# A GNN stack on one core: SpMM units cut into quarters between build batches, and zero fills issued by GpSimd

## The reference

```python
h = features * norm_out[:, None]
h = h @ W
agg = jax.ops.segment_sum(h[edge_src], edge_dst, num_segments=N)
gcn_out = agg * norm_in[:, None] + b
```

## Time and profile before

| | us |
|---|---|
| runs (3) | 2879.76, 2882.3, 2882.7; median 2882.3 |
| profiled execution, its span | 3131.6 |
| first build matmul to last SpMM matmul, in the profile | 88 to 503 |
| mean granted TensorE clock over the span | 0.771 |
| TensorE busy, share of the span | 69% |

### The profile page before, as it was taken

The page is one execution under the profiler, slowest core; times in us unless marked ns, Lnnn a source line. Parts: engine busy times, 40 slices in busy tenths (PEclk is TensorE's granted clock), DMA queues, the critical chain, the costliest instruction groups (busy, mean ns, idle before and its releaser), DMA issues.

```text
span 3131.6 us, 33483 instructions
## 1 busy us (share of the span) xinstructions
PE 2171.3 (69%) x10859; PEld 1508.0 (48%) x10859; DVE 1424.4 (45%) x3094; ACT 961.2 (31%) x2148; POOL 1362.2 (43%) x1417
## 2 busy tenths in 40 slices
PE   4899999468777777545666676682443443489998
PEld 3566667257666666332333333352333332356666
DVE  6766663646665655633444444332222222431414
ACT  3523321422233332553433443241222222220302
POOL 3000000666666663466666665257666666300000
PEclk9777778767888887768888888695555555599999
DMA  9479862277777885125666676314444554456361
GB/s 217 126 268 317 280 210 73 85 198 227 223 226 224 231 226 146 26 62 168 215 210 218 196 216 202 115 44 100 117 116 110 120 125 105 142 168 197 116 202 48
DMA packets 518583, 517.97 MB, mean 165 GB/s; under 512 B 153344, under 2 KB 463763, under 8 KB 517227
## 3 DMA queue, kind: packets, MB, share of 16 engines
q1 hardware_dynamic: 310349, 267.63, 28.1%
q0 software_dynamic: 50528, 115.22, 14.6%
q10 hardware_dynamic: 157534, 132.98, 13.7%
HBM read 301.53 MB, written 227.32 MB: 169 GB/s over the span
## 4 chain that ended last, share of the span: by engine, by line
PE 38%; another core or an unknown queue 15%; issue 14%; POOL 11%; DVE 9%; DMA 7%; ACT 6%; ACTq 1%; SPq 0%; POOLq 0%; DVEq 0%
PE ps L1577 9%; POOL arena L1047 9%; PE ps L1480 6%; PE ps L1470 6%; PE ps L1670 5%; ACT arena L1078 4%; DMA ends_gat<-arena 3%; DMA ends_attn<-arena 2%; PE ps L1559 2%; PE ps L1610 1%; PE ps L1620 1%; DVE arena L1988 1%; PE ps L1848 1%; DVE arena L2338 1%
## 5 line engine op out<-in xcount | busy, mean ns | idle before, releaser
L1078 ACT ACTIVATE arena<-ps 128x774 f32<-128x774 f32 (+8 forms) x689 | 496.8, 729 | 1548.0 <-remote 674.3
L1047 POOL DMA_INDIRECT arena<-t_gat,src_i x784 | 741.5, 946 | 373.1 <-issue 221.0
L1670 PE MATMUL ps<-arena 128*128 128x136 f32 (+2 forms) x2352 | 703.7, 460 | 283.0 <-ACT arena L1078 153.1
L1670 PEld LDWEIGHTS ps<-arena 128*128 128x128 f32 x2352 | 468.7, 265 | 449.4 <-issue 240.3
L1047 POOL DMA_INDIRECT arena<-t_attn,src_i x392 | 378.4, 965 | 211.9 <-issue 106.6
L1577 PE MATMUL ps<-arena 128*128 128x384 bf16 x1850 | 305.4, 329 | 34.3 <-issue 25.2
L1577 PEld LDWEIGHTS ps<-arena 128*128 128x128 bf16 x1850 | 182.0, 99 | 157.5 <-issue 40.2
L2338 DVE TENSOR_TENSOR arena<-arena,ps 128x1536 f32<-128x1536 f32 (+1 forms) x196 | 230.2, 1216 | 53.8 <-ACT arena L1217 35.6
L2322 DVE TENSOR_TENSOR dif<-logit,ps 128x64 f32<-128x64 f32 (+2 forms) x147 | 27.5, 187 | 459.3 <-remote 340.4
L1628 PE MATMUL ps<-ident,logit 128*64 128x128 f32 (+2 forms) x147 | 49.3, 335 | 265.5 <-issue 161.1
L1480 PE MATMUL ps<-arena 128*128 128x100 bf16 x1176 | 222.6, 364 | 10.9 <-DVE arena L2118 10.6
(11 more groups left out here) (321 smaller groups left out, 2833.7 us busy)
## 6 DMA issues: line engine op xcount, KB each, us to landing
ends_gat<-arena ACTq DMA_DIRECT2D x98, 774.0 KB
arena<-adj_hbm SPq DMA_DIRECT2D x90, 640.0 KB
same_b<-same_hbm SPq DMA_DIRECT2D x294, 128.0 KB
adj_hbm<-arena SPq DMA_DIRECT2D x9, 3200.0 KB, 12.4
ends_attn<-arena ACTq DMA_DIRECT2D x98, 272.0 KB
ends_gat<-arena ACTq DMA_DIRECT2D x98, 258.0 KB
arena<-edst SPq DMA_DIRECT2D x98, 256.0 KB, 4.8
starts_q<-zrow SPq DMA_DIRECT2D x28, 896.0 KB, 6.8
```

What stands on the lines that cost most here:

```text
L1047: g.indirect_dma_start(out=row_b[:, n % RB, k, 0:row_tab[p].shape[1]], out_offset=None, in_=row_tab[p], in_offset=bass.IndirectOffsetOnAxi ...
L1078: return a.activation(o, i, ACT.Copy)
L1670: i = mm(o, same_f[:, g % RB, k, :], msg[:, g % 4, k * W:(k + 1) * W], start=True, stop=True)
```

## The change

The SpMM unit is cut into quarters of 6, 6, 6 and 7 matmuls. One quarter stands behind each batch from 17 on. The splits are made one batch earlier, the fold of unit n moves from batch 21+4n to 23+4n, and the zero fills are issued by GpSimd, right after its gathers.

```diff
-SPLIT_AT = {"hi": 4, "r1": 7, "mid": 7, "r2": 9}
+SPLIT_AT = {"hi": 3, "r1": 6, "mid": 6, "r2": 8}
+PER_UNIT = PER // DG
+FOLD_AT = PER + 7
...
-                if g >= 10 and g % 2 == 0 and g // 2 - 5 < ZERO_PARTS:
-                    zeros(starts["attn"], ZERO_PARTS, g // 2 - 5, 256)
-                elif g in (71, 73):
-                    p = ("gat1", "gat2")[(g - 71) // 2]
-                    zeros(starts[p], 1, 0, 392)
...
             g.memset(xs0[:, :, 3 * D:XW], 1.0).then_inc(s_ones, 1)
+            (zeros as before, with pool.dma_start for sp.dma_start)
+            for part_at in range(ZERO_PARTS):
+                zeros(starts["attn"], ZERO_PARTS, part_at, 256)
+            for p in ("gat1", "gat2"):
+                zeros(starts[p], 1, 0, 392)
...
-            def spmm(ch, dl):
+            def spmm(n, t0, t1):
...
+            def quarter(k):
+                return k % PER_UNIT * NT // PER_UNIT, (k % PER_UNIT + 1) * NT // PER_UNIT
...
-                if b >= PER + 3 and b % 8 == 3:
-                    if b == PER + 3:
-                        pe.wait_ge(keys_t, 4)
-                    for n in range((b - PER - 3) // 4, (b - PER - 3) // 4 + 2):
-                        spmm(n // DG, n % DG)
+                if b > PER:
+                    k = b - PER - 1
+                    spmm(k // PER_UNIT, *quarter(k))
...
-            for n in range((NB - PER - 2) // 4, UNITS):
+            for k in range(NB - PER - 1, (UNITS - 1) * PER_UNIT + 1):
+                n = k // PER_UNIT
...
-                if b >= PER + 5 and b % 4 == 1:
+                if b >= FOLD_AT and (b - FOLD_AT) % PER_UNIT == 0:
```

More of the change, by code:

```diff
@@ L738, in store_adj @@
                 sp.dma_start(o, i).then_inc(adj_out[ch % 2], 16)
[L740 to L746, removed]
             sp.wait_ge(step_idx, 1)
@@ L983, in _, with zeros @@
             g.memset(xs0[:, :, 3 * D:XW], 1.0).then_inc(s_ones, 1)
+            def zeros(t, parts, at, wide):
+                n = EP * t.shape[1] // P // parts
+                flat = t[0:EP, :].rearrange("(b p e) c -> b p (e c)", b=parts, p=P)
+                pool.dma_start(flat[at].rearrange("p (a n) -> p a n", n=wide),
+                             zrow[:, 0:wide].rearrange("p (a n) -> p a n", a=1).to_broadcast([P, n // wide, wide]))\
+                  .then_inc(s_zero, 16)
+            for part_at in range(ZERO_PARTS):
+                zeros(starts["attn"], ZERO_PARTS, part_at, 256)
+            for p in ("gat1", "gat2"):
+                zeros(starts[p], 1, 0, 392)
             gt = g.tensor_tensor
@@ L1458, in _ @@
             keys_of(0, SOON, 0, 1)
-            def spmm(ch, dl):
[L1461 to L1468, removed]
+            def spmm(n, t0, t1):
+                ch, dl = n // DG, n % DG
+                if t0 == 0:
+                    pe.wait_ge(adj_done, min(NB, (ch + 1) * PER))
+                    if n == 0:
+                        pe.wait_ge(keys_t, 4)
+                        pe.wait_ge(dve_o.sem, dve_o.at("n0", "r2"))
+                        pe.wait_ge(s_ones, 1)
+                    if n >= 4:
+                        pe.wait_ge(v_done, n - 3)
+                for t in range(t0, t1):
                     lhs = adj[:, ch % 2, t * DG + dl, :] if ch < NC - 1 else adj_end[:, t * P:(t + 1) * P]
                     i = mm(bank(4 + n % 4)[:, 0:3 * D + 1], lhs, xs0[:, t, 0:3 * D + 1], start=t == 0, stop=t == NT - 1)
-                i.then_inc(spmm_done, 1)
+                if t1 == NT:
+                    i.then_inc(spmm_done, 1)
+            def quarter(k):
+                return k % PER_UNIT * NT // PER_UNIT, (k % PER_UNIT + 1) * NT // PER_UNIT
             pe.wait_ge(keys_t, 2)
@@ L1509, in _ @@
                         degrees(ch)
-                spmm(n // DG, n % DG)
+                    spmm(n, 0, NT)
+                else:
+                    spmm(n, *quarter(k))
             pe.wait_ge(v_done, UNITS)
```

## The result

The kernel after takes 2912.0 us (2911.1 to 2914.7, 4 runs) against 2882.5 for the kernel before in the same comparison: a ratio of 1.0094 [1.0071, 1.0116], 29.5 us slower. The prediction was 2859, 23 us faster. It was wrong in sign, and it missed by 53 us. Both halves of the change can be seen in the profile after, and they pull apart.

What follows compares the result with a forecast made beforehand. TensorE's builds and SpMM matmuls were taken to bound the adjacency stage, its clock falling between bursts. Gains of 24 + 2 less 1.1 and 2 gave 23 us: 2882.3 to 2859 us, range 2847 to 2886.

Steps and rivals of the forecast that it cites:

- The clock term: SpMM in the build loop: bursts pay 28.1 us for slow-clock matmuls; quarters keep the high clock, 24 us gained net.
- the stall: Build loop: VectorE's ring of three one-hot batches now covers the shorter SpMM pieces, 2.0 us gained.
- the splits: Node-table splits needed by batch 17, one batch earlier, with VectorE setting the pace until then: 1.1 us lost.
- a slow start over four quarters: First quarters from batch 17: 25 matmuls at the low clock level, 0.156 us extra each, 4 us charged.
- Rival B: Loop batches 17 to 146: clock stays low or swings; 2916 us at half the matmuls slow, 2980 at all; chance 0.14.
- Fold and tail: Later folds and the SpMM tail after the last build: hidden, with 1.6 us to spare; no cost.
- The zero fills: Fills moved to GpSimd from 56 us: cost between nothing and some 20 us through SP's backlog; 2 us taken.
- rival C: Around batches 25 to 48: fills delay SP's loads, VectorE and ScalarE wait, 10 to 22 us back, 2875 us; chance 0.14.
- If the fills took half, the 28 us left would be 56: Edge-feature copy on SP: sharing the DMAs with the fills, its remaining 28 us would double to 56.
- just covered: SP's later weight loads, mask and adjacency stores: each delay is just covered, so 2 us, near the lower end.
- The time at which 26 MB move: Fill traffic moves from 56 us instead of 171 to 395 us, beside the edge-feature copy; named as not free.
- 3131.6 against 2882.3: Profiled span against median of the runs, 8.6% apart; microseconds carried over unscaled, as this stage was judged not stretched.

Runs made afterwards that it cites:

- quarters_sp: The kernel after with the zero fills put back on SP where they were before: 2856.4 us, ratio 0.990 against the kernel before.
- ctl: The kernel before, unchanged, run again for a second profile: 2882.0 us.
- The three comparisons: Against the kernel before: the kernel after (1.0094), the kernel after with fills back on SP (0.990), the kernel before with only the fills moved to GpSimd (1.0167).
- the doses: The kernel after with 14 or 7 of the 28 large fills issued at once, the others paced by build batches: 2879.2 and 2860.5 us.
- paced: The kernel after with GpSimd's large fills let go one for every four build batches: 2859.0 us, ratio 0.9891 against the kernel before.
- copy_rows: The kernel after with the edge features copied in long runs, row reversal left out: 2885.5 us median (2879 to 2909), ratio 0.999 against the kernel before.
- quarters_pool_late: The kernel after with GpSimd's fills held until SP's early loads have landed: 2880.7 us, ratio 0.998 against the kernel before.

## Why the prediction was wrong, point by point

- **The clock term, 28.1 - 4 = 24 us, and the stall, +2, less 1.1 for the splits**: right. Their sum is 24.9; `quarters_sp` measures 28.7 (24 to 34 by its interval). The sum is measured; no run takes the terms of 2 and 1.1 apart. The 4 us charged for a slow start over four quarters were nearly all too much: one quarter is slow, 1.93 us for 0.99. Rival B (a clock that stays low or swings) did not come; it does come with coarser grain. The rule of the Trainium skill, "TensorE: Matmul & The Clock Gate", section "A second HAM failure mode: psum-queue depth-cycling", that groups of matmuls with brief pauses between them swing and lose, describes the swing seen there, not its cause: between these groups stand thin matmuls, and TensorE never pauses. For quarters the trace does not show the swing: 1.00.
- **Fold and tail, nothing**: right. No SpMM matmul of `quarters_sp` waits for a fold (one matmul behind them does, 1.3 us, and as long in `ctl`), and the last SpMM matmul comes at 454.8, 28.3 us before that of `ctl`.
- **The zero fills, "I take 2", bound "some 20 us"**: this step failed. The three comparisons put their cost at 56 to 58 us behind quarters and 49 behind bursts. The place and the chain (SP's backlog reaches VectorE) were those of rival C, with 0.14; only its price, 10 to 22 us, was as wrong as mine. The sentence that failed is "If the fills took half, the 28 us left would be 56". I took the turn by packets to mean half of the bytes. The fills took sixteen of seventeen parts of what the two moved, as their packets are sixteen times as long; what SP had left waited for all 26 MB, 74 us. The rows shown had no packet sizes, though the page of the profile counts packets by size.
- **The delays that were "just covered"**: the cover exists, 12 to 18 us by the doses. With the delay at 28 us, as I had it, the cost would have been 10 to 16, not 2; that much was mis-sized even with my halving.
- **"The time at which 26 MB move"** was named as the thing not free, and that was so: the same fills from the same engine cost 0 to 3 us paced (`paced`), 24 in one lump from 106 us, 56 in one lump from 57.8.
- **3131.6 against 2882.3**: carrying microseconds over from an unrepresentative execution did no harm: the terms came from this stage, and as the prediction argued from its 0.164 us a matmul, that execution ran it at nearly its usual pace (a burst takes 9.96 us there and 9.86 in `ctl`).

The change without its fills, or with the fills paced, beats both kernels: 2856.4 and 2859.0 us.

What stays open: why `copy_rows` spreads over 30 us from run to run, what makes up the rest of the cover, and why 14 fills made VectorE wait three times as long as expected. The halves of the change together cost 9 us more than their sum; the three intervals, of 5 to 6.5 us to either side, leave room for no difference at all, and the stages differ by 2 us only (53 and 50 us longer).

## What to carry to other kernels

Before a transfer is moved in time, ask which queues are busy then, how long the packets of each are, and who reads what they bring. Where queues share the DMAs, the one with small packets falls to the ratio of the packets, not to a half (here 0.75 MB beside 12.01): its delay is the other's bytes over the full rate, less what its own equal number of packets would have taken. Bulk writes that nobody waits for are best paced by the work they run beside: behind the small loads, but in one lump, they still cost 24 us here. And the dense matmuls are best spread finely between the thin ones: here builds in pieces of 1.5 us kept TensorE at its high level, and pieces of 2.9 and 5.9 us did not.

## What the hardware showed beyond that

- A plain transfer of 896 KB costs GpSimd 0.95 us to issue, SP 0.52. But after 17 of them GpSimd stood for 37 us before the next, 51 us in `quarters_pool_late`: with work behind them on GpSimd, that would be a cost of its own.
- The same fills leave GpSimd's queue in packets of 4 KB, and SP's in 1 KB (10,680 of the 13,931 packets of `quarters_sp` between 180 and 240 us have 512 bytes to 2 KB).
- Long packets are no remedy: 61 KB ones held a load of another queue up for 47 us.
